# A chunked delta-rule layer with routed experts on one core: new orders on four engines, zeros while x loads, and a second expert tile in the ramp

## The reference, cut to what matters

```python
xn = layernorm(x)                                   # x: 2 x 2048 x 256
q = xn @ Wq * 128**-0.5                             # 4 heads of 128
k = xn @ Wk; k = k * rsqrt(sum(k*k) + 1e-12)
v = xn @ Wv; beta = sigmoid(xn @ Wb)                # v: 4 heads of 64
for t in range(2048):                               # per sequence and head
    S = S + k[t] (beta[t] * (v[t] - k[t]^T S))^T
    o[t] = q[t]^T S
o = o * rsqrt(mean(o*o) + 1e-5) * norm_w * silu(xn @ Wg)
s = o @ Wo
e = argmax(xn @ router_w^T)                         # one of 8 experts per token
y = relu(xn @ expert_fc[e])**2 @ expert_proj[e]^T   # 256 -> 1024 -> 256
out = x + s * silu(y)
```

## Time and profile before

| | us |
|---|---|
| median of 3 runs | 816.02 (815.68 to 816.42) |
| profiled execution, its own time | 813.94 |
| its span, first to last instruction | 812.2 |
| PE busy | 767.0 |
| DVE busy | 529.9 |
| POOL busy | 390.6 |
| ACT busy | 346.6 |

### The profile page before, as it was taken

One profiled execution on the slowest core, in us unless ns is written; L12 is line 12 of the kernel. 1 busy time (PEld: TensorE's weight loads), 2 busy tenths in 40 slices (PEclk: granted clock), 3 DMA queues, 4 the chain that ended last, 5 costly groups with the idle time before them and its releaser, 6 DMA issues.

```text
span 812.2 us, 21978 instructions
## 1 busy us (share of the span) xinstructions
PE 767.0 (94%) x8906; PEld 649.7 (80%) x8906; DVE 529.9 (65%) x1159; ACT 346.6 (43%) x754; POOL 390.6 (48%) x407
## 2 busy tenths in 40 slices
PE   4987899999999999999999999999999999999953
PEld 3874888888888889888888888878787878788942
DVE  5677565655756556575665746776767677767577
ACT  3823434444443445344444444444443534444420
POOL 5522473545526354363544625463647465564421
PEclk9998899999999999999999999999999999999965
DMA  9416534424343263333523343232333323140087
GB/s 305 156 47 244 192 121 174 176 111 176 132 162 125 112 229 124 117 125 143 209 111 133 131 176 149 112 124 112 124 112 118 118 101 136 53 184 8 21 275 249
DMA packets 37747, 116.24 MB, mean 143 GB/s; under 512 B 3664, under 2 KB 24400, under 8 KB 27664
## 3 DMA queue, kind: packets, MB, share of 16 engines
q1 hardware_dynamic: 33904, 104.62, 35.2%
q0 software_dynamic: 3744, 10.23, 3.9%
HBM read 101.33 MB, written 13.50 MB: 141 GB/s over the span
## 4 chain that ended last, share of the span: by engine, by line
PE 88%; DVE 4%; DMA 3%; POOL 2%; issue 1%; ACT 1%; SPq 0%; POOLq 0%; DVEq 0%
PE bank L453 18%; PE bank L464 17%; PE bank L529 7%; PE bank L497 7%; PE bank L482 7%; PE bank L427 4%; PE bank L429 4%; PE bank L428 4%; PE bank L668 4%; PE bank L564 3%; PE bank L574 3%; PE bank L584 3%; POOL ImM L2034 2%; PE bank L509 2%; PE bank L386 2%
## 5 line engine op out<-in xcount | busy, mean ns | idle before, releaser
L464 PE MATMUL bank<-wts,hT 128*128 128x256 f32 x624 | 173.0, 394 | 0.0
L453 PE MATMUL bank<-xsT,wts 128*128 128x128 f32 x1248 | 168.0, 282 | 0.2
L453 PEld LDWEIGHTS bank<-xsT,wts 128*128 128x128 f32 x1248 | 151.9, 193 | 11.0 <-issue 11.0
L1486 DVE TENSOR_TENSOR Pm<-bank,lvl_mask 128x256 f16<-128x256 f32 x192 | 72.6, 419 | 72.0 <-PE bank L564 71.1
L1029 ACT CAST Z<-bank 128x256 f16<-128x256 f32 x192 | 63.5, 376 | 120.9 <-PE bank L584 120.8
L2015 POOL TENSOR_TENSOR XTl<-f_t,XTh 128x512 f16<-128x512 f32 x32 | 40.1, 1262 | 151.7 <-DVE XTh L1429 151.7
L1497 DVE TENSOR_TENSOR M<-bank,M 128x256 f16<-128x256 f32 x192 | 73.6, 419 | 56.4 <-PE bank L574 55.7
L464 PEld LDWEIGHTS bank<-wts,hT 128*128 128x128 f32 x624 | 104.7, 191 | 6.8
L973 ACT ACTIVATE hT<-bank 128x512 f32<-128x512 f32 x78 | 46.7, 598 | 54.4 <-PE bank L453 54.4
L529 PE MATMUL bank<-wvg_sb,xT 128*128 128x512 f32 x128 | 64.5, 627 | 0.3 <-DVE gate L1448 0.3
L497 PE MATMUL bank<-xT,wq_sb 128*128 128x128 f32 x512 | 63.1, 276 | 0.0
(11 more groups left out here) (211 smaller groups left out, 1945.6 us busy)
## 6 DMA issues: line engine op xcount, KB each, us to landing
wts<-in_fc SPq DMA_DIRECT2D x39, 1024.0 KB, 4.8
wts<-in_pj SPq DMA_DIRECT2D x39, 1024.0 KB, 7.5
wts<-in_x SPq DMA_DIRECT2D x10, 512.0 KB, 9.2
wts<-y_d SPq DMA_DIRECT2D x4, 1024.0 KB, 10.1
out_x<-wts SPq DMA_DIRECT2D x16, 256.0 KB, 2.4
xn_d<-wts SPq DMA_DIRECT2D x3, 1024.0 KB, 4.4
x_first<-in_x SPq DMA_DIRECT2D x4, 512.0 KB, 12.0
wts<-in_x SPq DMA_DIRECT2D x4, 256.0 KB, 3.9
```

Of the source, the lines that this page charges most:

```text
L453: ins = pe.matmul(psum[bank[n]][:, (c % 4) * P:(c % 4 + 1) * P], fcw[r][:, k, c * P:(c + 1) * P], xsT[:, k, :], start=(k == 0), stop=(k == ...
L464: ins = pe.matmul(psum[bank[0]][:, 0:D], hT[:, c, :], pjw[r][:, c, :], start=(c == 0), stop=(c == HC - 1))
L1486: dve.tensor_tensor(h4(Pm, b).rearrange("p h (n c) -> p h n c", c=s), half4(b).rearrange("p h (n c) -> p h n c", c=s), mask, ALU.mult).the ...
```

## The change

The tiles of the ramp become two, and the steps seven of three tiles and seven of two. SP issues x's parts 1, 2, 3 and 4 ahead of wk, wq and wvg as shown. PE multiplies zeros (64 products of 128 x 128 x 128 in half precision, into a bank that later products overwrite) as soon as DVE has cleared S16, which DVE now does first. Chunk 0's Q(0,1), VG(0,0), VG(0,1) and kT move behind the logits of all chunks; POOL's rstd_of move between its constants. All lists of ramp, step3, step2 and tail have a new order on PE, ACT, DVE and POOL; the operations are the same, except for the zeros. The core of the diff, first constants, SP and PE:

```diff
+        WARM_UP = 64
         X_PARTS = [range(0, 2), range(2, 4), range(4, 8), range(8, 12), range(12, 16)]
-        FIRST_TILES, STEPS = 1, [3] * 8 + [2] * 6
+        FIRST_TILES, STEPS = 2, [3] * 7 + [2] * 7
...
                 load_x(0)
                 load_w(wbr_sb, wbr, wbr_in)
+                load_x(1)
                 load_w(wk_sb, wk, wk_in)
-                load_x(1)
+                load_x(2)
+                load_x(3)
                 load_w(wq_sb, wq, wq_in)
+                load_x(4)
                 load_w(wvg_sb, wvg, wvg_in)
-                for k in range(2, len(X_PARTS)):
-                    load_x(k)
                 load_w(wo_sb, wo, wo_in)
...
+                def warm_up():
+
+                    pe.wait_ge(s_zero, 2)
+                    zeros = S16[0][:, 0:2, :].rearrange("p h n -> p (h n)")
+                    for _ in range(WARM_UP):
+                        pe.matmul(psum[CH_BANK][:, 0:P], zeros, zeros, start=True, stop=True)
+
...
                 def ramp():
+                    warm_up()
                     turn(0)
                     turn(1)
+                    K(0, 0)
+                    turn(2)
+                    K(0, 1)
+                    turn(3)
...
-                    logits_of(3)
                     Q(0, 0)
                     turn(4)
+                    logits_of(2)
                     turn(5)
-                    K(0, 1)
+                    logits_of(3)
...
                     logits_of(6)
-                    turn(9)
-                    Q(0, 1)
                     logits_of(7)
-                    logits_of(8)
...
                     logits_of(14)
                     logits_of(15)
+                    kT(0, 1)
+                    kT(0, 0)
+                    G(0, 1)
                     G(0, 0)
-                    kT(0, 1)
-                    PTm(0, 0)
-                    VG(0, 1)
-                    G(0, 1)
                     ranks()
                     counts()
+                    PTm(0, 0)
+                    places()
+                    Q(0, 1)
+                    VG(0, 0)
                     M0(0)
-                    places()
-                    Q(1, 0)
                     L(0, 0)
                     K(1, 0)
+                    experts_of_tiles()
                     Dm(0, 0)
+                    PTm(0, 1)
+                    tokens_of_rows()
+                    T(0, 0)
+                    VG(0, 1)
+                    L(0, 1)
+                    K(1, 1)
+                    Q(1, 0)
+                    Dm(0, 1)
+                    T(0, 1)
+                    transpose_rows(0)
                     Q(1, 1)
-                    T(0, 0)
-                    L(0, 1)
-                    Dm(0, 1)
-                    experts_of_tiles()
-                    T(0, 1)
...
+                    experts(1)
+                    L(0, 2)
+                    experts(5)
+                    Dm(0, 2)
+                    experts(2)
+                    T(0, 2)
...
-                    transpose_rows(0)
+                    G(1, 0)
+                    G(1, 1)
                     T(0, 3)
+                    experts(3)
+                    L(0, 4)
+                    experts(4)
+                    Dm(0, 4)
                     experts(1)
-                    L(0, 4)
-                    experts(2)
-                    Dm(0, 4)
-                    experts(2)
+                    PTm(1, 1)
                     T(0, 4)
+                    PTm(1, 0)
                     experts(2)
                     L(0, 5)
+                    experts(4)
+                    Dm(0, 5)
+                    VG(1, 1)
                     experts(2)
...
                     T(0, 5)
-                    experts(1)
-                    kT(1, 0)
+                    experts(4)
                     F(0)
-                    G(1, 1)
-                    experts(1)
-                    G(1, 0)
+                    experts(4)
                     Zc(0)
-                    PTm(1, 1)
-                    experts(1)
-                    PTm(1, 0)
-                    experts(3)
...
                 def step3(i, t):
                     KS(i - 1)
+                    Q(i + 1, 0)
+                    experts(2)
+                    U(i - 1)
+                    experts(1)
+                    K(i + 1, 1)
                     K(i + 1, 0)
+                    experts(3)
+                    M0(i)
+                    experts(4)
+                    L(i, 0)
+                    O(i - 1)
+                    Dm(i, 0)
                     experts(6)
-                    U(i - 1)
-                    K(i + 1, 1)
+                    T(i, 0)
+                    Q(i + 1, 1)
                     experts(2)
-                    Q(i + 1, 0)
-                    M0(i)
-                    O(i - 1)
-                    L(i, 0)
-                    experts(4)
-                    Dm(i, 0)
-                    experts(1)
-                    Q(i + 1, 1)
                     dS(i - 1)
...
                     L(i, 4)
-                    experts(2)
+                    experts(1)
+                    PTm(i + 1, 0)
                     Dm(i, 4)
-                    experts(2)
+                    experts(3)
                     T(i, 4)
                     experts(2)
                     L(i, 5)
...
                 def step2(i, t):
                     KS(i - 1)
+                    K(i + 1, 0)
+                    experts(2)
+                    U(i - 1)
                     experts(3)
-                    K(i + 1, 0)
-                    experts(1)
-                    U(i - 1)
-                    experts(1)
-                    Q(i + 1, 0)
                     K(i + 1, 1)
                     M0(i)
...
                     T(i, 4)
+                    PTm(i + 1, 1)
                     experts(1)
                     L(i, 5)
-                    experts(1)
+                    experts(2)
                     Dm(i, 5)
+                    PTm(i + 1, 0)
                     experts(1)
                     T(i, 5)
+                    experts(1)
                     F(i)
                     experts(2)
                     Zc(i)
...
+                    L(15, 2)
+                    dS(14)
+                    experts(1)
+                    Dm(15, 2)
                     experts(2)
-                    L(15, 2)
+                    T(15, 2)
+                    experts(2)
+                    L(15, 3)
                     ogT_(14)
-                    experts(2)
-                    Dm(15, 2)
-                    wo(14)
-                    T(15, 2)
-                    KS(15)
-                    L(15, 3)
                     Dm(15, 3)
                     T(15, 3)
+                    wo(14)
                     L(15, 4)
                     Dm(15, 4)
+                    KS(15)
                     T(15, 4)
                     L(15, 5)
                     Dm(15, 5)
```

DVE, from choose to the first level, the end of step2, and the tail's middle:

```diff
+                    choose()
+                    X32(0, 1)
                     X32(0, 0)
-                    choose()
+                    X_h(0, 1)
                     X_h(0, 0)
                     count()
-                    MZ(0, 0)
-                    X32(0, 1)
-                    Zo(0, 0)
-                    X_h(0, 1)
-                    v(0, 1)
                     MZ(0, 1)
                     pad_counts()
+                    MZ(0, 0)
+                    place_rows()
+                    P32(0, 0)
                     Zo(0, 1)
-                    gate_(0, 1)
-                    P32(0, 0)
-                    place_rows()
+                    q_l(0, 1)
+                    rows_onehot(0)
+                    Zo(0, 0)
+                    tiles_onehot()
+                    past_tiles()
+                    tile_numbers()
                     Pm_(0, 0, 0)
                     Pm_(0, 0, 1)
-                    q_l(1, 0)
-                    tiles_onehot()
+                    rows_onehot(1)
+                    v(0, 0)
+                    keep_experts()
+                    gate_(0, 0)
                     dM(0, 0, 0)
                     dM(0, 0, 1)
-                    rows_onehot(0)
+                    P_h(0, 0)
+                    keep_tokens()
+                    P32(0, 1)
+                    P_h(0, 1)
+                    v(0, 1)
+                    gate_(0, 1)
+                    Pm_(0, 1, 1)
+                    kss_(1, 0)
                     Pm_(0, 1, 0)
-                    past_tiles()
-                    Pm_(0, 1, 1)
-                    q_l(1, 1)
+                    kss_(1, 1)
                     dM(0, 1, 0)
-                    keep_experts()
                     dM(0, 1, 1)
-                    rows_onehot(1)
-                    tile_numbers()
...
+                    P32(i + 1, 1)
                     P32(i + 1, 0)
-                    P_h(i + 1, 1)
+                    v(i + 1, 1)
                     Fr_(i, 0)
                     Fr_(i, 1)
+                    P_h(i + 1, 1)
```

(28 more changed lines are left out.)

549 lines of the change are left out of this document (264 added, 285 removed).

## The result

The changed kernel takes 833.06 us, the median of four runs (828.65, 830.57, 835.55, 835.70), against 815.85 for the kernel before in the same comparison: a ratio of 1.0213, 95% interval 1.0184 to 1.0243. It is slower by 2.1% (whether by more than 2% the interval leaves open), where I forecast 803 and gave slower a chance of 0.08. The four runs lie 7 us apart, and their mean granted TensorE clock falls with the time: 0.966, 0.963, 0.957, 0.955.

A forecast was written before the change was run, and what follows sets the result against it. TensorE's own work was taken to bound the kernel, with room only in the ramp and last stretch. Ramp −0.9, steps −10.0 and last stretch −2.0 sum to −12.9, so 816.02 becomes 803.1 us, range 794 to 813.

The forecast's parts named there:

- Load stretch, up to choose: Ramp until routing begins: earlier x, higher clock and moved products start choose at 37.0 instead of 46.76, −9.8 us.
- 16 turns at 0.5, 16 logits at 0.85: Load stretch: TensorE's work at the higher clock, 27.0 us with two K and one Q, ending at 36.2.
- cold load rival: Load stretch: zeros' higher clock is lost again in the turns; +4.5 us on the forecast, 808; chance 0.14.
- choose to KS(0): Rest of the ramp: gather issued at +23.6, first expert at +33.2 (−4.5 us), then 29.4 to KS(0) (+13.4).
- Steps: Seven three-tile steps at 49.09 and seven two-tile at 42.10: 638.3 us against 648.4, −10.0; bounds −6.5 and −11.5.
- The three-tile step has nothing to gain: Three-tile steps: the new order leaves each at 49.09 us.
- Two-tile steps did gain what I forecast: Two-tile steps: the 0.28 wait before F and Zc's longer time go, 0.51 us gained, 42.61 to 42.10.
- slower rival: Steps: VectorE's casts, stretched beside GpSimd's passes, cost 1.6 us a step, 22 in all, giving 825; chance 0.07.
- U, whose margin held: Steps: margin before U falls from 1.8 to 0.2 us; rival of a late U costs 9.8, 813; chance 0.15.
- Last stretch: End of the kernel: Pm(15,5) ahead of weigh(0) no longer waits for y; −2.0 us, bounds −3.5 and +1.
- the chain F, U, O, wo that ends the kernel moves by about 2: Last stretch: Pm starts at about 778, so the closing chain moves by about 2 us.
- The small terms, x's loads and the zeros: Load stretch: x's part 2 comes 3 us earlier; 7 us of zeros hide behind loading, some 4.5 returns if useless.

The follow-up runs named there:

- e1_ramp: The kernel before with the change's ramp and split into seven and seven steps, but before's orders in steps and last stretch: 820.83 us, ratio 1.0025.
- e18_after_fill: The changed kernel plus one product of zeros of 384 columns ahead of each logits_of from chunk 4 on: 822.78 us, ratio 1.0141.
- e21_after_fill3: The changed kernel plus three products of zeros of 384 columns ahead of each logits_of from chunk 4 on: 823.37 us, ratio 1.0115.
- e9_split: Change's ramp with three products of zeros per logits_of from chunk 4; change's steps with expert units moved; O(14), dS(14) behind the last expert unit: 814.39 us, ratio 0.9997.
- e2_steps: The kernel before with only the change's two step orders, keeping its own ramp and last stretch: 827.09 us, ratio 1.014.
- e4_tail: The kernel before with only the change's orders of the last stretch: 815.32 us, ratio 1.0002.
- e22_best2: Change's ramp with two products of zeros per logits_of from chunk 4, before's three-tile steps and last stretch, change's two-tile steps edited: 807.86 us, ratio 0.9944.

## Why the prediction was wrong

**Load stretch, up to choose: −9.8 forecast, −0.9 measured.** The term that failed is "it has, at the higher clock, 16 turns at 0.5, 16 logits at 0.85". I had the prices of both clocks in hand and assumed that a busy TensorE keeps the higher one. The zeros at the start I did weigh, as the cold load rival, but that rival lost only the start, though the page's rule named beside it would have held for every turn; what fell was the clock after 24 to 31 us. 15.4 us at 0.5 before choose cost half of that, 7.7: 45.9 − 7.7 = 38.2; e1_ramp gives 52.2 − 13.8 = 38.4, e18_after_fill 40.6 less 2 for its products. The last 1.3 over 37.0 goes with the start, as far as the rows tell: VectorE's first memset is at 4.03, not at the 1.7 that I took, and the first turn at 11.51, not 9.2. That the moved work hides in the routing was right: choose to KS(0) takes 62.9, forecast 62.6 (+23.6 to the gather was +25.3, and the rest 1.4 shorter). With the fall ended, the changed kernel is 10 us faster, for all that it has 6 us of zeros more (e21_after_fill3).

**Steps: −10.0 forecast, +4.6 measured.** "The three-tile step has nothing to gain" was true and half of the matter: with 0.24 us idle in 393, a new order has next to no wait to win and can still bring new ones. It lost 0.31 at M0 and 0.86 by TensorE's lag, which the trace of before did not hold and whose cause stays open. Two-tile steps did gain what I forecast (no wait before F, Zc at its short time) and lost more at M0: 1.18. The stretched pass of the slower rival is real, at 2.09 against 0.45, but I had put it on U, whose margin held (one wait of 0.16 at U in fourteen steps), and looked at no other place where VectorE's list meets GpSimd's. The mend is worth 43.00 − 41.62 = 1.4 a step.

**Last stretch: −2.0 forecast, +1.7 measured.** The step that failed is "the chain F, U, O, wo that ends the kernel moves by about 2". I freed Pm(15,5) from the wait for y, but the new order has dM(15,5), two links on, behind weigh(0): TensorE waits 3.9 there where it waited 2.3 for Pm(15,5), and the chain still starts with y's arrival. Counted from the first weigh, dM(15,5) is done 2.1 sooner than before, R_h for U 1.0 sooner (weighings and R_l stand between now), and the end comes 0.3 sooner: VectorE, idle for 2.0 us in all from the first weigh to its last addition, has little to give. Nineteen traces, e9_split's aside, end 31.6 to 32.2 us after the first weigh, from 63.2 to 65.4 us of stretch. And y itself came later: it was asked for 27.3 after KS(14) instead of 25.6, and the first weigh is 2.0 later. Neither the steps' orders alone (e2_steps, 26.0) nor the last stretch's alone (e4_tail, 26.0) do that; with both it is 27.3 in all six traces, and in e22_best2 too, which has before's last stretch. What holds the last y back is not shown.

The small terms, x's loads and the zeros, came out near nothing, as in the sum. The forecast's sum with the three stretches as measured is the 14.7 of the profile; 4 us more stand between profile and median, and the other runs had a lower mean clock still.

## What to carry to other kernels

A matmul engine that is 100% busy with transposes and narrow products can still lose its clock: before moving wide products from among them to where they hide for nothing, count them as what holds the clock, and try a few wide products of zeros in their place. Where a stretch has no idle time, ask of a new order first what it can lose, at every place where two engines' lists meet, not at the one with the smallest margin. And when an edit seems to mend something, run the unedited order in the same surroundings too: two edits here seemed to mend a lateness that the unedited order did not have either in such a run.

## What was not expected of the hardware

- The granted clock fell to 0.50 for 20.5 us (from 30.5) and 30.7 us (from 24.6) with TensorE busy without a gap before and for all but 0.3 us of what was read of them; by the times and mean clocks of the runs of one kernel it happens in some executions and not in others (e1_ramp: 811 to 816 and 821 to 824).
- 36 products of zeros of 384 columns (6 us) kept it at 1.00 to choose in three profiles of four (in e9_split it is 0.50 for 6.8 us from 25.5), 24 in the one that had them, 12 in three of four. They make the long falls rarer; they don't end them for certain.
- TensorE signalled 1.0 to 1.9 us behind its modelled ends after G(i+1,0) and PTm(i+1,1), at the same place in every three-tile step, in some traces and not in others with identical steps: 50.27 against 49.24 us a step. The cause is open.
- VectorE's addition of two SBUF tiles took 2.09 us instead of 0.45 where GpSimd's P_l started 0.6 us into it, and 1.85 where P_l started 0.4 us into it: both times it ended 0.3 us after P_l. Beside GpSimd's issue of a store alone it took 0.45.
